# Causal masks taken from TensorE's matmuls and put into VectorE's maxima and a GpSimd select

## The reference

```
h = layernorm(x) * (1 + ca) + sa
q = rotary(h @ Wq + bq)   # 16 heads of 64
k = rotary(h @ Wk + bk)   # 4 heads of 64, each shared by 4 query heads
v = h @ Wv + bv
logits = q k^T / 8
logits = where(causal, logits, -1e30)      # query i sees keys 0..i
out = softmax(logits) @ v  -> @ Wo + bo
x = x + ga * out
```

## Time and profile before

| | |
|---|---|
| time, median of 3 | 1443.35 us (1442.36 to 1443.93) |
| profiled execution, span from first to last instruction | 1441.1 us |
| attention loop, one of its four turns | 260.5 us (326.5 to 587.0 us is one) |
| TensorE busy | 1325.4 us, 92% |
| VectorE busy | 953.8 us, 66% |
| ScalarE busy | 588.5 us, 41% |
| GpSimd busy | 563.4 us, 39% |

### The profile page before, as it was taken

How to read it: one execution, slowest core, us unless ns; L and a number is a source line. 1 busy time by engine, 2 the same in 40 slices (tenths; PEclk the granted TensorE clock), 3 DMA queues, 4 the chain that set the end, 5 groups by cost and what they waited for, 6 DMA issues and landing times.

```text
span 1441.1 us, 19077 instructions
## 1 busy us (share of the span) xinstructions
PE 1325.4 (92%) x6864; PEld 834.6 (58%) x6864; DVE 953.8 (66%) x1834; ACT 588.5 (41%) x1229; POOL 563.4 (39%) x541
## 2 busy tenths in 40 slices
PE   3699999987999998799999879999995699999998
PEld 2455555544555554455555445555543588888888
DVE  4677777676787776668777676877778644444444
ACT  2444544543454453444444444444453322232222
POOL 4454347353444645345445414644643301111110
PEclk9799999999999999899999989999998699999999
DMA  5000000000000000000000000000001001010101
GB/s 128 1 1 1 1 1 0 2 0 2 1 0 1 0 1 0 2 1 1 1 1 1 0 1 1 1 1 0 1 0 44 0 7 39 0 40 4 29 16 30
DMA packets 18449, 13.02 MB, mean 9 GB/s; under 512 B 7104, under 2 KB 15680, under 8 KB 18368
## 3 DMA queue, kind: packets, MB, share of 16 engines
q1 hardware_dynamic: 11072, 9.58, 2.3%
q10 hardware_dynamic: 7296, 2.36, 0.7%
HBM read 10.88 MB, written 1.05 MB: 8 GB/s over the span
## 4 chain that ended last, share of the span: by engine, by line
PE 77%; DVE 14%; issue 3%; POOL 3%; ACT 1%; ACTq 1%; SPq 0%; DVEq 0%; POOLq 0%; another core or an unknown queue 0%
PE PS L1046 16%; PE PS L1105 12%; PE PS L999 11%; PE PS L1027 10%; PE PS L1119 8%; PE PS L1029 8%; DVE k_split L761 2%; PE PS L975 2%; PE PS L1055 2%; PE PS L1064 2%; PE PS L1012 2%; DVE full L788 2%; DVE part_max L772 2%; PE PS L983 2%; DVE q_split L758 1%
## 5 line engine op out<-in xcount | busy, mean ns | idle before, releaser
L772 DVE TENSOR_REDUCE part_max<-PS 128x1 f32<-128x512 f32 (+2 forms) x576 | 348.8, 620 | 127.6 <-PE PS L999 103.0
L601 ACT ACTIVATE full<-PS 128x512 f32<-128x512 f32 x384 | 224.9, 598 | 231.2 <-PE PS L1029 215.5
L1027 PE MATMUL PS<-QT,KT 128*128 128x512 f32 (+3 forms) x640 | 271.4, 424 | 20.4 <-issue 18.7
L999 PE MATMUL PS<-KT,QT 128*128 128x512 f32 (+3 forms) x656 | 273.0, 429 | 10.0 <-ACT QMT L581 4.7
L1029 PE MATMUL PS<-QMT,KT 128*128 128x512 f32 (+3 forms) x640 | 237.7, 371 | 0.0
L999 PEld LDWEIGHTS PS<-KT,QT 128*128 128x128 f32 x656 | 127.2, 197 | 158.4 <-DVE part_max L772 74.1
L464 POOL TENSOR_TENSOR full<-full 128x2048 f32<-128x2048 f32 x32 | 145.7, 4576 | 173.7 <-PE PS L1046 173.0
L610 ACT ACTIVATE diag<-PS 128x512 f32<-128x512 f32 (+3 forms) x256 | 111.3, 437 | 243.5 <-PE PS L1032 217.1
L1046 PE MATMUL PS<-full,V 128*64 128x512 f32 x768 | 210.2, 626 | 0.0
L494 POOL TENSOR_TENSOR rot_cos<-qkv_sb,cos_sb 128x320 f32<-128x320 f32 x72 | 69.9, 970 | 335.0 <-DVE qkv_sb L748 332.6
L1027 PEld LDWEIGHTS PS<-QT,KT 128*128 128x128 f32 x640 | 125.8, 197 | 106.0 <-issue 39.0
(11 more groups left out here) (116 smaller groups left out, 1748.3 us busy)
## 6 DMA issues: line engine op xcount, KB each, us to landing
full<-in_L_ffn_experts_w_dram SPq DMA_DIRECT2D x24, 256.0 KB, 3.1
out_dram<-XA SPq DMA_DIRECT2D x4, 256.0 KB, 2.3
wqkv<-in_L_attn_Wq_dram ACTq DMA_DIRECT2D x1, 512.0 KB, 4.0
bqkv<-in_L_attn_bq_dram ACTq DMA_DIRECT2D x1, 512.0 KB, 9.3
wo_sb<-in_L_attn_Wo_dram SPq DMA_DIRECT2D x1, 512.0 KB, 8.8
sin_sb<-in_k_sin_dram ACTq DMA_DIRECT2D x1, 512.0 KB, 8.2
full<-in_L_wmod_dram SPq DMA_DIRECT2D x1, 384.0 KB, 9.2
cos_sb<-in_k_cos_dram ACTq DMA_DIRECT2D x1, 256.0 KB, 9.1
```

The lines of the kernel that those rows point to most:

```text
L601: nc.scalar.activation(full[:, k % QUADS, r, :], PS[:, bank, :], ACT.Exp).then_inc(probs_ready, 1)
L772: nc.vector.reduce_max(part_max[:, t, b:b + 1], PS[:, bank, 0:width], AX.X).then_inc(ring_dve, 1)
L999: last = nc.tensor.matmul(PS[:, bank, 0:w], QT[:, ch % 2, h, t * P:(t + 1) * P], KT[:, 0, b * BANK:b * BANK + w], start=True, stop=not las ...
L1027: nc.tensor.matmul(o, KT[:, 0, kt * P:(kt + 1) * P], QT[:, ch % 2, h, q0:BANK], start=True, stop=False)
```

## The change

- The two mask matmuls (L1002, L1032), `ident16` and `causal16` go.
- The maximum of a diagonal tile becomes one `tensor_tensor_reduce`: it adds a bf16 mask from SBUF to the scores in PSUM, writes the sum back to PSUM and takes the maximum (chunk 0: the minimum of the negated sum) on the way.
- A new item "tri" on GpSimd, once per J and r: an `affine_select` sets to zero the exponentials above the diagonal, in the corners of both heads (2 x 128 columns), in place in `diag`.
- "pv" of a diagonal tile waits for its "tri" and stands two steps behind its "s" instead of one. The sums of the diagonal wait for the last "tri".
- The first GpSimd sum of steps J = 4 and 5 moves behind the last "tri" (in J = 2, 3 the order is as it was), a window of `place` moves for J = 6, and each "s" of the diagonal waits for the "pv" of its own r of the step before.
- `best` and `tok_sum` move into other memory.

```diff
-        "k_causal": np.stack([np.where(col <= row, 0.0, MASKED), np.where(row <= col, 0.0, MASKED)], 1)
-        .astype(np.float32),
+        "k_causal": np.concatenate([np.zeros((P, BANK - P)), np.where(col <= row, 0.0, MASKED)], 1).astype(np.float32),
...
+    starts_at = np.cumsum([0] + [TB * (J // PAIRS + 1) for J in PAIR_STEPS])
     for J in PAIR_STEPS:
         starts.append(len(main))
         for q in range(J // PAIRS + 1):
             for r in range(TB):
-                main += [("s", J, q, r, 0), ("s", J, q, r, 1)] + pending
+                step_of = TB * q + r + starts_at[J]
+                main += [("s", J, q, r, 0), ("s", J, q, r, 1)]
+                main += [x for due, x in pending if due <= step_of]
+                pending = [(due, x) for due, x in pending if due > step_of]
                 if r == 0 and q > 1:
-                    if q < CHUNKS - 1:
+                    if q == J // PAIRS < CHUNKS - 1:
+                        pass
+                    elif q < CHUNKS - 1:
                         main += [("poolsum", J, m, q - 1) for m in range(2)]
                     else:
                         main += [("quadsum", J, m, part) for m in range(2) for part in range(4)]
-                pending = [("pv", J, q, r)]
+                if q == J // PAIRS:
+                    main.append(("tri", J, r))
+                    pending.append((step_of + 2, ("pv", J, q, r)))
+                    if r == TB - 1 and q == 2:
+                        main += [("poolsum", J, m, q - 1) for m in range(2)]
+                else:
+                    pending.append((step_of + 1, ("pv", J, q, r)))
...
-        place(diag_steps(6) + tail_steps(6), 7.0, 7.48),
+        place(diag_steps(6) + tail_steps(6), 7.07, 7.5),
...
+                    elif x[0] == "tri":
+                        _, J, r = x
+                        pool.wait_ge(probs_ready, n.at["s", J, J // PAIRS, r, 1] + 1)
+                        corner = diag[:, :, r, r * P:(r + 1) * P]
+                        nc.gpsimd.affine_select(corner, corner, [[0, 2], [1, P]], ALU.is_ge, 0.0, base=0,
+                                                channel_multiplier=-1).then_inc(diag_masked, 1)
...
-                        pool.wait_ge(probs_ready, n.at["s", J, ch, TB - 1, m] + 1)
+                        pool.wait_ge(diag_masked, n.at["tri", J, TB - 1] + 1)
...
+                    if J > 0:
+                        act.wait_ge(pv_done, n.at["pv", J - 1, (J - 1) // PAIRS, r] + 1)
                     if r == 0 and J > 0:
-                        act.wait_ge(pv_done, n.at["pv", J - 1, (J - 1) // PAIRS, TB - 1] + 1)
...
                     if ch == 0:
-                        nc.vector.tensor_reduce(q_max[:, 0, t, 2 * (J % PAIRS) + m, HEAD:HEAD + 1],
-                                                PS[:, bank, 0:width], AX.X, ALU.max, negate=True).then_inc(ring_dve, 1)
+                        nc.vector.tensor_tensor_reduce(out=scores, in0=scores, in1=causal_max[:, BANK - width:BANK],
+                                                       scale=-1.0, scalar=-MASKED, op0=ALU.add, op1=ALU.min,
+                                                       accum_out=q_max[:, 0, t, 2 * (J % PAIRS) + m, HEAD:HEAD + 1])\
+                          .then_inc(ring_dve, 1)
+                    elif b == ch:
+                        nc.vector.tensor_tensor_reduce(out=scores, in0=scores, in1=causal_max[:, BANK - width:BANK],
+                                                       scale=1.0, scalar=MASKED, op0=ALU.add, op1=ALU.max,
+                                                       accum_out=part_max[:, t, b:b + 1]).then_inc(ring_dve, 1)
...
-                        dve.wait_ge(probs_ready, n.at["s", J, ch, TB - 1, m] + 1)
+                        dve.wait_ge(diag_masked, n.at["tri", J, TB - 1] + 1)
...
-                    if last_bank:
-                        last = nc.tensor.matmul(PS[:, bank, w - P:w], ident16[:], causal16[:, 0, :],
-                                                start=False, stop=True)
...
-                    if q == ch:
-                        last = nc.tensor.matmul(PS[:, bank, q0:q0 + P], ident16[:], causal16[:, 1, :],
-                                                start=False, stop=True)
...
-                    need(probs_ready, n.at["s", J, q, r, 1] + 1)
+                    if q == ch:
+                        need(diag_masked, n.at["tri", J, r] + 1)
+                    else:
+                        need(probs_ready, n.at["s", J, q, r, 1] + 1)
```

More of the change, by code:

```diff
@@ L89, in weight @@
             return part * (3.78 if x[0] == "max" else 2.0)
-        return {"pv": 2.1, "qmax": 1.5, "proj": 3.0, "low": 3.0, "qk": 3.5, "poolsum": 0.01, "maxed": 0.25,
+        return {"tri": 0.0, "pv": 2.1, "qmax": 1.5, "proj": 3.0, "low": 3.0, "qk": 3.5, "poolsum": 0.01, "maxed": 0.25,
                 "diagsum": 3.3, "quadsum": 0.01, "sum": 2.8, "rowsum": 12.6, "norm": 2.8, "modulation": 0.0,
@@ L170, in block_kernel @@
     closing = tail_steps(-1)
-    body = [("values",)] + merge([(float(b), x) for b, x in zip(before, main)], [(begin[end], x) for x in pending],
+    body = [("values",)] + merge([(float(b), x) for b, x in zip(before, main)], [(begin[end], x) for _, x in pending],
                                  *side)
@@ L288, in block_kernel @@
         wmod_sb = full[:, 1].rearrange("p a b -> p (a b)")[:, 0:6 * E]
-        causal = full[:, 2, 0, 0:2 * P].rearrange("p (a b) -> p a b", b=P)
+        causal = full[:, 2, 0, :]
         silu_c, bo_sb, gate_bo = (full[:, 2, 1, n * P:(n + 1) * P] for n in range(3))
@@ L306, in block_kernel @@
                                .rearrange("p (t x) -> p t x", x=NX) for n in range(3))
-        best = sb("best", [P, TILES])
-        tok_sum = sb("tok_sum", [P, TILES])
+        best, tok_sum = (full[:, 5, 3, 3 * TILES * NX + n * TILES:3 * TILES * NX + (n + 1) * TILES] for n in range(2))
         tok_wT = sb("tok_wT", [P, NX, TILES])
@@ L996, in step @@
                     bank = ring_bank(x)
-                    last_bank = b == ch
-                    w = (t + 1) * P if last_bank else BANK
-                    last = nc.tensor.matmul(PS[:, bank, 0:w], QT[:, ch % 2, h, t * P:(t + 1) * P],
-                                            KT[:, 0, b * BANK:b * BANK + w], start=True, stop=not last_bank)
-                    if last_bank:
-                        last = nc.tensor.matmul(PS[:, bank, w - P:w], ident16[:], causal16[:, 0, :],
-                                                start=False, stop=True)
-                    last.then_inc(ring_filled, 1)
+                    w = (t + 1) * P if b == ch else BANK
+                    nc.tensor.matmul(PS[:, bank, 0:w], QT[:, ch % 2, h, t * P:(t + 1) * P],
+                                     KT[:, 0, b * BANK:b * BANK + w], start=True, stop=True).then_inc(ring_filled, 1)
                 elif kind == "qmax":
@@ L1028, in step @@
                                      start=True, stop=False)
-                    last = nc.tensor.matmul(o, KT[:, 1, kt * P:(kt + 1) * P], QMT[:, h, q0:BANK],
-                                            start=False, stop=q < ch)
-                    if q == ch:
-                        last = nc.tensor.matmul(PS[:, bank, q0:q0 + P], ident16[:], causal16[:, 1, :],
-                                                start=False, stop=True)
-                    last.then_inc(scores_ready, 1)
+                    nc.tensor.matmul(o, KT[:, 1, kt * P:(kt + 1) * P], QMT[:, h, q0:BANK],
+                                     start=False, stop=True).then_inc(scores_ready, 1)
                 elif kind == "pv":
```

12 lines of the change are left out of this document (6 added, 6 removed).

## The result

The changed kernel takes 1466.25 us (median of 4, 1465.57 to 1468.15), the kernel before 1443.33 in the same measurement. The ratio is 1.0155, 95% interval [1.0141, 1.0169]: 23 us slower, where 1417 us (1393 to 1452) was forecast. The prediction was wrong in its direction.

The account below looks back on a forecast made before the run. The prediction took TensorE to bound the attention turn, apart from some 15 us. Its terms summed to -6.3 us per turn, -25.2 over four turns and -1.6 in the lead-in, about -27: 1417 us, range 1393 to 1452.

Parts of the forecast that it names:

- masks off TensorE: On TensorE: 128 mask matmuls leave each turn at 0.10 us each, -12.8 us per turn.
- masked maximum: On VectorE: 64 per turn, each 0.1 us longer than the plain maximum, felt as +0.5 us per turn.
- turn's start: GpSimd's queue at J = 0: two selects come between rotations and sums that ScalarE's exponentials await, +1.0 us.
- J = 4 and 5: Quad sums start behind the last select, so VectorE's sums wait; +2 us per turn for both.
- J = 6: At J = 6, quad sums hold VectorE's q_split, the first select waits behind rotation 19, TensorE idles: +8 us per turn.
- J = 7: At J = 7, low20 ahead of the quad sums lets q_split run first: -6.8 us per turn.
- turn's end, selects: First select of J = 7 waits for rotation 23, four selects share the port with VectorE's sums: +1.8 us.
- new order, two steps of delay: Moved waits, such as earlier "pv" semaphores, were costed at nothing because they release no later than before.
- Even without the collision +3: At J = 6, the select would still wait for the rotation until 527.2, past its due "pv": +3 us.
- the rival built on it (1397): No collision at J = 6: the quad sums miss low17, the place costs 3 and not 8; chance 0.18.
- The rival of the long select: On GpSimd: selects from 1.0 us on make the change slower, 1459 us at 1.3 us each; chance 0.14.
- signs of its mechanism: Masked maximum row 0.69 to 0.86, select 0.35 to 0.76; split over 4 us at J = 6, at most one at J = 7.

Follow-up runs that it names:

- e1: The kernel before with both mask matmuls left out, list order unchanged: 1392.76 us, ratio 0.9653.
- e9: The kernel after without its selects; new order, two steps of delay and masked maxima kept: 1401.03 us, ratio 0.97.
- e2: The kernel before without the 272 masks of the maxima, plain maxima over unmasked scores: 1410.59 us, ratio 0.9762.
- e3: The kernel before with the masked maximum only, second-pass masks and list order kept: 1410.29 us, ratio 0.9768.
- e7: The kernel after with plain maxima over unmasked scores instead of masked ones: 1459.73 us, ratio 1.0101.
- g2: e9 with the quad sums of J = 4 and 5 held back to the last exponential: 1408.21 us, ratio 0.9754.
- e8: The kernel before with low20 moved ahead of the two quad sums of J = 7, masks kept: 1428.51 us, ratio 0.9892.
- e5: The kernel after with low17 moved ahead of the quad sums of J = 6: 1454.67 us, ratio 1.0076.
- e6: As e5, with the first select of J = 6 and of J = 7 also ahead of the rotation: 1432.63 us, ratio 0.9929.
- g1: As e6, but three selects moved at J = 6 and only the first at J = 7: 1419.77 us, ratio 0.9839.
- e10: The kernel after with each select over 2 x 2 instead of 2 x 128 elements: 1456.48 us, ratio 1.0079.
- g3: As g1, but at J = 7 proj23 is moved forward instead of the first select: 1412.12 us, ratio 0.9784.
- f2: e6 with the first three selects of both J ahead of the rotation, low20 ahead of max8120, and plain maxima: 1434.41 us, ratio 0.993.

## Why the prediction was wrong

The sum had -6.3 us per turn, the turn became 5.7 longer. Term by term, from the differences of e1, e9 and the kernel after in the table:

| term | forecast | measured | from |
|---|---|---|---|
| masks off TensorE | -12.8 | -8.1 | e1: -4.95 for 52 from J = 4 to J = 7 chunk 1, -3.1 for 56 in J = 0 to 3, none for the last 20 |
| masked maximum | +0.5 | 0 (1.1 to 1.9 in the kernel after) | e2, e3; e7 |
| turn's start | +1.0 | +0.6 | after less e9, J = 0 to 3 |
| J = 4 and 5 | +2 | +2.1 | g2; after less e9 |
| J = 6 | +8 | +9.4 | after less e9 |
| J = 7 | -6.8 | -6.7 | e1; -7.2 in e8 |
| turn's end, selects | +1.8 | +3.3 | after less e9 |
| turn's end, once J = 7 is shorter | none | +1.6 | e1; +2.1 in e8 |
| new order, two steps of delay | 0 | +3.0, masked maxima included | e9 less e1 |

The remaining 0.4 of the selects lies in J = 4 to 7, outside these places. No single term turns the sign: some 12 us per turn were missing, spread over four places. What I had for the selects was nearly right, 12.8 us per turn (turn's start, J = 4 and 5, J = 6, turn's end) against 15.8 measured.

- **The step that failed first is that the masks' time comes back in full.** The price was right: 0.10 us taken, 0.095 measured where TensorE never idles. But I let all 128 through. In J = 0 to 3 TensorE idles 7.6 us a turn, and 56 masks brought 3.1 us there instead of 5.6, because its idle time rose to 9.5. The last 20 masks of a turn bring nothing that can be seen: in J = 7 chunk 2 e8, with its masks, is as short as e1, and the end of the turn waits for VectorE. Together the error is 4.7 us per turn, 19 in all.
- **Costed at nothing, and wrongly: the new order.** "GpSimd is free; nothing" held for the selects of J = 2 and 3 (0.6 in all of J = 0 to 3). But with the products two steps late and the list shifted the turn is 3.0 us longer even with no select. Some of it can be the masked maxima: they cost nothing in the order of before (e2, e3), 1.1 to 1.9 us per turn in the changed kernel (e7), and no run has the new order without both selects and masked maxima. It isn't idle time of TensorE, and I have not traced it to single instructions. How e9 less e1 lies over the stretches says little: four product matmuls and a wait of 1.7 us for VectorE's maxima only change sides of a line in J = 7.
- **The end of the turn** took 4.9 us and not 1.8. Of them 1.6 come in e1 and, with all masks in place, in e8 (2.1): when J = 7 got shorter, what VectorE still had to do did not. The prediction named VectorE there and then let all of the gain through.
- **J = 6 was right in mechanism and nearly in price**: 6.5 us of idle time forecast, 6.94 seen, first select forecast behind rotation 19. But I weighed the parts wrongly. Of 9.4 us, the collision with low17 brought 2.9 (e5), and the queue place of the first select 3.4 and of the next two 3.1 (e6, g1). "Even without the collision +3" should have been +6.5, and the rival built on it (1397) was too fast by that.
- **J = 7 was right in number, and its cause is one of two.** In the changed kernel the move of low20 puts q_split 0.53 us ahead, and the move alone also brings the gain (e8). But so do the missing masks alone, by 0.06 us (e1, e2, e3). Booked as a gain of the change it hid that the rest of the change loses 12 us per turn; a one-line edit (e8) collects it alone.
- **The rival of the long select** fell by its own row, 503 ns. A shorter select gives 10 us (e10), and moving five items with the selects at full length gives 54 (g3).
- **The signs.** All that the prediction named as signs of its mechanism came true: the two new rows, the long operations at J = 6, at most one at J = 7. What came as well is its last sign of being wrong, a turn that isn't shorter all the same. The chance given to slower was 0.19, most of it (0.14) for the long select, so for a reason that did not come.

The trace agrees that the masked maximum is two instructions (the Trainium skill, VectorE: DVE Perf Modes, "Two Vector instructions with no wait between them"): 272 accumulator reads of 140 ns are in it. Most of them overlap other VectorE work, so they add only 7 of the 38 us by which its busy time rises, 953.8 to 991.9; q_split and k_split, held by quad sums, add 17 and the sums in `full` 14.

## What to carry to other kernels

An instruction of half a microsecond on an idle engine is not free if TensorE waits for it. It ties TensorE to everything ahead of it in that engine's queue, so list what stands there at each of its places. Count the clock too: at J = 6 the waits of 2.71 (e6), 3.94 (e5) and 6.94 us were followed by matmuls at half speed, though one of 2.89 us at the turn's end of f2 was not. Time taken off an engine comes back in full only in the stretches where it never idles (here 0.095 us for each mask, but 0.056 in J = 0 to 3), so forecast it by stretch. A collision between two engines costs nothing until someone on the critical path waits behind it: price the waiter, not the collision. And before a stall that disappears is booked as a gain of a change, ask by how much its race was lost; if by 0.1 us, try the smallest edit that turns it round.

## What the runs showed of the hardware

- An index select on GpSimd over 128 x 256 float32 took 0.41 us (median) and over 128 x 4 0.19 (e10), which as an estimate is 0.9 ns per element on a start of 0.19. Of the 128 selects, the 63 with no two-operand addition of VectorE beside them took 0.41 us each; the 65 with one took 0.59 on average, the longest 0.90 (the three at 535.20 above took 2.27 us together).
- A masked maximum that reads PSUM and one SBUF operand and writes all columns back to PSUM took the same 0.69 us over 512 columns as a plain maximum, and never more than 0.70 in the 192 executions of L792. Twenty of these ran beside a quad sum, none of them over 512 columns, and were as long as the others of their width (0.57 us over 384). q_split and k_split, with two SBUF operands, took 3.55 to 4.61 us beside the quad sums, against 0.41 and 0.21 alone. The Trainium skill (SBUF — State Buffer, "Who interferes with whom") says the same: with at most one SBUF input VectorE doesn't contend with GpSimd (outside the modes that use two ports), and with two SBUF inputs it contends with a GpSimd instruction that reads SBUF, for a port pair that is an exclusive lock.
- A 128x128 bf16 matmul that is listed with 0.237 us costs 0.095 in the stream where TensorE never idles, two fifths of its row.
